# Attention of a gated two-layer block: queries and own keys turned by transposing DMAs, scores for the maximum moved later in the step

## The reference

```python
qkv = (_layernorm(x) @ w_qkv.T)            # 16 heads of 8 columns: q, k, v
k, v = concat([ctx_k, k]), concat([ctx_v, v])   # 64 context rows, then the 64 own rows
attn = softmax((q * 8 ** -0.5) @ k.T)      # for each sequence and head
x = x + tanh(g_xattn[0]) * ((attn @ v) @ w_proj.T + b_proj)
```

## Time and profile before

| | us |
|---|---|
| median of 3 runs | 507.96 (507.57 to 509.46) |
| profiled execution, its own time | 503.36 |
| its span | 501.8 |
| first and last L1525 of the attention | 8.0 and 203.5 |

### The profile page before, as it was taken

How to read it: one execution, slowest core, us unless ns; L and a number is a source line. 1 busy time by engine, 2 the same in 40 slices (tenths; PEclk the granted TensorE clock), 3 DMA queues, 4 the chain that set the end, 5 groups by cost and what they waited for, 6 DMA issues and landing times. The chain is left out here.

```text
span 501.8 us, 21152 instructions
## 1 busy us (share of the span) xinstructions
PE 456.2 (91%) x6983; PEld 359.6 (72%) x6984; DVE 374.9 (75%) x1201; ACT 286.5 (57%) x803; POOL 319.6 (64%) x780
## 2 busy tenths in 40 slices
PE   5799999999999999997987999987998699999998
PEld 3467777766666766764647888874656599998997
DVE  3668989988888989854649766654656688888984
ACT  2378999987888888764324444433333344444431
POOL 3845764576768776756722556667834888988530
PEclk9899999999999999999989999997999699999999
DMA  7930000000000000000144677751000011111001
GB/s 233 413 127 14 27 15 5 5 14 14 12 11 6 11 12 11 14 16 17 58 139 125 189 225 225 224 159 33 22 12 6 22 34 42 37 37 37 22 23 33
DMA packets 22539, 33.62 MB, mean 67 GB/s; under 512 B 5592, under 2 KB 16656, under 8 KB 21968
## 3 DMA queue, kind: packets, MB, share of 16 engines
q0 software_dynamic: 7552, 20.20, 12.6%
q1 hardware_dynamic: 14352, 12.39, 7.6%
q10 hardware_dynamic: 576, 0.26, 0.2%
HBM read 24.82 MB, written 7.86 MB: 65 GB/s over the span
## 5 line engine op out<-in xcount | busy, mean ns | idle before, releaser
L947 DVE TENSOR_REDUCE negm<-PS 128x4 f16<-128x512 f32 x128 | 81.9, 681 | 5.4 <-PE PS L1332 3.0
L689 ACT ACTIVATE pexp<-PS 128x512 f32<-128x512 f32 x128 | 69.6, 595 | 16.1 <-PE PS L1348 12.7
L1684 PE MATMUL PS<-w,vp 128*128 128x128 f32 x512 | 64.0, 279 | 0.0
L1684 PEld LDWEIGHTS PS<-w,vp 128*128 128x128 f32 x512 | 61.2, 196 | 0.0
L1361 PE MATMUL PS<-pexp,vp 128*32 128x64 f32 x2048 | 49.9, 224 | 2.2 <-ACT pexp L689 1.1
L1578 PE MATMUL PS<-xsT,wst 128*128 128x128 f32 x320 | 44.3, 282 | 2.6 <-DVE stack L1185 1.3
L1361 PEld LDWEIGHTS PS<-pexp,vp 128*32 128x32 f32 x2048 | 33.8, 109 | 16.5 <-issue 7.4
L1578 PEld LDWEIGHTS PS<-xsT,wst 128*128 128x128 f32 x320 | 38.8, 191 | 7.0 <-issue 6.0
L584 POOL DMA_DIRECT2D wst<-in_rt_gate_up_dram x40 | 21.6, 540 | 32.6 <-PE PS L1578 22.1
L554 POOL DMA_INDIRECT sorted_x<-VALL,posu x32 | 32.8, 1026 | 13.8 <-issue 8.3
L1278 DVE TENSOR_TENSOR vp<-PS,xnT 128x1024 f32<-128x1024 f32 x32 | 38.7, 1209 | 1.2 <-PE PS L1661 1.2
(11 more groups left out here) (245 smaller groups left out, 1287.8 us busy)
## 6 DMA issues: line engine op xcount, KB each, us to landing
wst<-in_rt_gate_up_dram POOLq DMA_DIRECT2D x40, 256.0 KB, 3.5
xs<-sorted_x SPq DMA_DIRECT2D x40, 64.0 KB, 2.8
sorted_y<-YS POOLq DMA_DIRECT2D x40, 64.0 KB, 3.0
qc<-mT SPq DMA_DIRECT2D x128, 1.0 KB
out_dram<-X SPq DMA_DIRECT2D x32, 64.0 KB
X<-in_x_dram SPq DMA_DIRECT2D x1, 1536.0 KB, 8.8
CK<-in_ctx_k_dram SPq DMA_DIRECT2D x1, 1536.0 KB, 12.0
CV<-in_ctx_v_swapped_dram SPq DMA_DIRECT2D x1, 1536.0 KB, 16.7
```

The costliest lines, as they stand in the source:

```text
L689: nc.scalar.activation(pexp[:, j, :], PS[:, 2 + j % 2, :], ACT.Exp).then_inc(S["exped"], 1)
L947: dve.tensor_reduce(negm[:, a.par, :, j], PS[:, j % 2, :].rearrange("p (g k) -> p g k", g=G), AX.X, ALU.max, negate=True).then_inc(S["maxe ...
L1684: nc.tensor.matmul(PS[:, 6 + y.par, 0:D], z[:, y.par, e, :], w1[:, e * D:e * D + D], start=(e == 0), stop=False)
```

## The change

`turned_on_pe(tile)` is true for the first four tiles. From tile 4 on the queries and the own keys are turned by three transposing DMAs on SP's queue instead of TensorE, and the copies L715 and L986 fall away. The semaphores `stack_turned` take the place of `q_kept`, `k_kept` and `qk_turned`; the next write of the same `stack` buffer (two tiles later) waits for them. The context keys are turned earlier in TensorE's step, into bank 5, and copied between the exponentials. The four small DMAs of the maxima become one. The semaphores of the last three input loads become one.

The order in the step changes too. On TensorE half 0 of the scores for the maximum moves from the step's start to just ahead of the q, k, v matmul; half 1 moves from there to just ahead of the transposes of `oS`; the transpose of the maxima goes behind the first scores by key. On VectorE maxima 0 and 1 go from the start of the step to just ahead of the reciprocal, and maxima 2 and 3 behind the write of the remainder.

```diff
+        def stack_seen(eng, tile):
+            eng.wait_ge(stack_turned[tile.par], 48 * (tile.pair - 1))
+        def stack_freed(eng, tile):
+            if not (tile.turn is None and tile.n < 6):
+                eng.wait_ge(stack_turned[tile.par], 48 * (tile.pair - 2))
...
# SP
+            def turn_stack(s):
+                sp.wait_ge(S["hi_ready"], s.done())
+                sp.wait_ge(S["lo_ready"], s.done())
+                sp.wait_ge(S["scored_t"], s.freed(4, 3, back=16))
+                sp.nop(nofuse=True)
+                sp.dma_start_transpose(qc[:, s.slot], stack[:, s.par, 0, 0:H, :].rearrange("p h c -> p (h c)"))\
+                    .then_inc(stack_turned[s.par], 16)
+                for b in range(2):
+                    own = stack[SEQ * b:SEQ * b + SEQ, s.par, 1, 0:H, :].rearrange("p h c -> p (h c)")
+                    sp.dma_start_transpose(own_half(s.slot)[:, b], own).then_inc(stack_turned[s.par], 16)
             def step(stage):
-                a = stage(3)
+                s, a = stage(1), stage(3)
+                if s and not turned_on_pe(s):
+                    turn_stack(s)
                 if a:
                     sp.wait_ge(S["max_kept"], a.done())
-                    for hg in range(HG):
-                        sp.dma_start(qc[32 * hg + 24:32 * hg + 25, a.slot, :, :],
-                                     mT[HG * hg:HG * hg + G, a.par, :]).then_inc(shift_placed[a.par], 16)
+                    sp.dma_start(qc[24:P:32, a.slot, :, :], mT[:, a.par, :]).then_inc(shift_placed[a.par], 16)
...
# VectorE
-                if a:
-                    max_chunk(a, 0)
-                    max_chunk(a, 1)
                 if l:
...
                 if a:
-                    max_chunk(a, 2)
-                    max_chunk(a, 3)
+                    max_chunk(a, 0)
+                    max_chunk(a, 1)
                 if n:
                     dve.wait_ge(S["o_turned"], n.done())
...
+                if a:
+                    max_chunk(a, 2)
+                    max_chunk(a, 3)
                 if c:
...
# TensorE
-                if a:
-                    scores_for_max(a, 0)
...
                 if a:
-                    scores_for_max(a, 1)
+                    scores_for_max(a, 0)
...
                 if b:
                     average(b, 1)
+                if a:
+                    scores_for_max(a, 1)
                 if n:
```

More of the change, by code:

```diff
@@ L306, in by_seq, with turned_on_pe @@
             return bank.rearrange("p (g b t) -> p b g t", g=G, b=2)
+        def turned_on_pe(tile):
+            return tile.turn is None and tile.n < 4
+        def stack_seen(eng, tile):
[3 more added lines that the diff above has]
+                eng.wait_ge(stack_turned[tile.par], 48 * (tile.pair - 2))
         def bank16(b):
@@ L312, in flamingo_gated_two_layers @@
         TILE_CHUNKS = [(0, 2), (2, 8), (8, NT)]
-        x_in = [sem(f"x_in{c}") for c in range(3)]
-        ck_in = [sem(f"ck_in{c}") for c in range(3)]
-        cv_in = [sem(f"cv_in{c}") for c in range(3)]
+        rest_in = sem("rest_in")
+        x_in = [sem(f"x_in{c}") for c in range(2)] + [rest_in]
+        ck_in = [sem(f"ck_in{c}") for c in range(2)] + [rest_in]
+        cv_in = [sem(f"cv_in{c}") for c in range(2)] + [rest_in]
         consts_in = sem("consts_in")
@@ L331, in flamingo_gated_two_layers @@
         shift_placed = [sem("a_shift_placed0"), sem("a_shift_placed1")]
+        stack_turned = [sem("a_stack_turned0"), sem("a_stack_turned1")]
         for n in "stats moments var_eps copied normed kept xnT_done xnT_kept routed".split():
@@ L383, in arrived @@
                     if tile.n == lo:
-                        eng.wait_ge(sems[c], 16)
+                        eng.wait_ge(sems[c], 16 if c < 2 else 48)
                         eng.nop(nofuse=True)
@@ L700, in step @@
                     if not (w.turn is None and w.n < 2):
-                        act.wait_ge(shift_placed[w.par], 64 * w.pair)
+                        act.wait_ge(shift_placed[w.par], 16 * w.pair)
                     act.wait_ge(S["max_turned"], w.done())
@@ L712, in step @@
                     nc.scalar.copy(xnT[:, f.par, :], PS[:, 4, 0:P]).then_inc(S["xnT_kept"], 1)
-                if s:
+                if s and not turned_on_pe(s):
+                    act.wait_ge(S["ctx_turned"], s.done())
+                    last = nc.scalar.copy(ctx_half(s.slot), by_seq(bank16(5)[:, 0:512]))
+                    last.then_inc(S["ctx_kept"], 1)
+                elif s:
                     act.wait_ge(S["qk_turned"], s.done())
@@ L719, in step @@
                     exp_chunk(b, 3)
-                if s:
+                if s and turned_on_pe(s):
                     act.wait_ge(S["ctx_turned"], s.done())
@@ L724, in step @@
                 if f:
-                    act.wait_ge(S["qk_turned"], f.freed())
+                    if f.turn is None and f.n < 6:
+                        act.wait_ge(S["qk_turned"], f.freed())
+                    stack_freed(act, f)
                     act.wait_ge(S["qkv_done"], f.done())
@@ L782, in gates_in_drain @@
                     shared_gate(3, 1)
-            walk(act, NT, 12, step, lambda: act.wait_ge(ck_in[2], 16), drain=gates_in_drain)
+            walk(act, NT, 12, step, lambda: act.wait_ge(rest_in, 48), drain=gates_in_drain)
             act.wait_ge(S["h_acted"], Tile(EARLY - 1).done(2, 1))
@@ L1052, in products_in_drain @@
                     shared_product(1, 1)
-            walk(dve, NT, 13, step, lambda: dve.wait_ge(x_in[2], 16), drain=products_in_drain)
+            walk(dve, NT, 13, step, lambda: dve.wait_ge(rest_in, 48), drain=products_in_drain)
             chained = [0]
@@ L1323, in scores_for_max @@
                 if half == 0:
-                    pe.wait_ge(S["q_kept"], a.done())
-                    pe.wait_ge(S["k_kept"], a.done())
+                    if turned_on_pe(a):
+                        pe.wait_ge(S["q_kept"], a.done())
+                        pe.wait_ge(S["k_kept"], a.done())
+                    else:
+                        stack_seen(pe, a)
                     pe.wait_ge(S["ctx_kept"], a.done())
@@ L1340, in scores_by_key @@
                 if half == 0:
-                    pe.wait_ge(shift_placed[b.par], 64 * (b.pair + 1))
+                    pe.wait_ge(shift_placed[b.par], 16 * (b.pair + 1))
                 pe.wait_ge(S["exped"], b.freed(4, 2 * half + 1, back=2))
@@ L1440, in step @@
                 past = ro.n + 13 - NT if ro and ro.turn is None else -1
-                if a:
-                    scores_for_max(a, 0)
-                if a:
+                if a and turned_on_pe(a):
                     pe.wait_ge(S["ctx_kept"], a.done())
@@ L1454, in step @@
                     nc.tensor.transpose(PS[:, 6, 0:P], on[:, m.par, :], identf).then_inc(S["on_turned"], 1)
+                if b:
+                    if b.turn is None and b.n == 0:
+                        keep_busy(14, 7)
+                    scores_by_key(b, 0)
                 if c:
@@ L1458, in step @@
                                         ident16[:]).then_inc(S["max_turned"], 1)
[L1459 to L1463, removed]
+                if s and not turned_on_pe(s):
+                    pe.wait_ge(S["ctx_stacked"], s.done())
+                    turn_stack(s, 2, 5, 0, "ctx_turned")
+                elif s:
                     if s.turn is None and s.n == 0:
@@ L1537, in step @@
                     average(b, 1)
+                if a:
+                    scores_for_max(a, 1)
                 if n:
                     pe.wait_ge(S["o_kept"], n.done())
-                    if s:
+                    if s and not turned_on_pe(s):
+                        pe.wait_ge(S["ctx_kept"], s.done())
+                    elif s:
                         pe.wait_ge(S["k_kept"], s.done())
@@ L1544, in step @@
                     last.then_inc(S["o_turned"], 1)
-                if s:
-                    if s.turn is None and s.n < 3:
+                if s and turned_on_pe(s):
+                    if s.n < 3:
                         keep_busy(5, 7)
```

## The result

The changed kernel takes 584.38 us (median of 4 runs, 577.0 to 592.35) against 508.71 us for the kernel before beside it. Forecast were 542 us. The time lies just inside the range of 525 to 585 us, but the loss is 76 us where 34 were forecast.

What follows compares the result with a forecast made beforehand. The attention was taken as bound by TensorE before and by a 7.33 us chain of waits after; 13.5, 17.8 and 2.4 us added 34 to 503.4, giving 537 us profiled and 542 us median, range 525 to 585.

Steps and rivals of the forecast that it cites:

- The ring: Attention steps: one chain of waits through TensorE, VectorE and ScalarE sets the pace, 7.33 us a step; chance 0.76.
- The waits: Per attention step: VectorE about 1 us ahead of the reciprocal; TensorE 0.4 ahead of half 1, about 1.3 later.
- The sum at full clock: Steps 6 to 34: 13.5 us lost in ten written-out steps, 17.8 in sixteen loop steps, 2.4 at the end; 33.7 together.
- the drain: The two steps after the loop: 1.2 us lost in each, 2.4 us together.
- the last rival, the clock: TensorE in the attention: pauses halve its clock in stretches, 29 steps growing by up to 100 us; chance 0.02.
- The sign for it: TensorE's busy share from 48 to 96 us would fall from 99% to under 85%.
- a kernel bound by its DMAs: Rival on SP's queue: issue of the three transposes over 5.8 us decides, 572 to 640 us; chance 0.12.
- The DMAs: SP's three transposing DMAs a tile: about 3 us of issue, hidden, with no wait for them.
- The limit behind it: SP's queue: the maxima's small DMA follows the transposes, whose issue may take up to 5.8 us a tile.
- No gain from TensorE's saved work: TensorE in the attention: the 0.45 us a step saved on transposes of q and k buys nothing.

Runs made afterwards that it cites:

- The order alone: Kernel before with only the changed order of scores and maxima, q and k still turned on TensorE: 557.29 us against 492.86, 1.128.
- the order back: Changed kernel with scores for the maximum, their maxima and the maxima's transpose in the old order, transposing DMAs kept: 506.8 us, 1.023 of the kernel before.
- the output first: Changed kernel with only the transposes of the output moved ahead of half 1 of the scores: median 551.72 us.
- With fillers: Changed kernel plus 12 idle matmuls ahead of the transpose of the maxima and 4 ahead of half 1: 535.28 us, 1.087 of the kernel before.
- half 0 in between: Changed kernel, DMAs kept, half 0 behind the first scores by key, the rest ordered as before: 504.16 us, 1.017 of the kernel before.

## Why the prediction was wrong

- **The ring: right.** Summed from the trace of before it was 7.33 us a step; the changed kernel took 7.12 us at full clock. This isn't errors that cancel: the links measure 0.46 us (0.53 in the sum), 1.34 (1.34), 1.04 (1.04), 0.84 (0.83), 1.33 (1.34) and, from the turned maxima to the next half 0, 2.11 (0.85 + 1.40). The order alone took 7.25 us, and 7.33 once the router's matmul is in the step as it is in the rows summed. The waits came where they were named: 1.09 us ahead of the reciprocal (about 1 forecast), 0.19 us ahead of half 1 (0.4), 0.86 + 0.23 us ahead of the turned maxima and the context transposes (1.3). One reading was wrong without consequence: in the step of the earlier trace rows ScalarE waited twice and not once, 0.18 us and 0.25 us for the context keys (L722). That the order and not the DMAs makes the ring is shown by the order alone (7.25 us), the order back, and the output first (0.60 us less).
- **The sum at full clock: nearly right.** 33.7 us were forecast. With fillers, the loss was 42.4 us by the medians and 38.7 us by the spans of the two traces (532.4 and 493.7 us), which can be divided. The q, k, v matmuls of tiles 5, 15 and 31, with fillers (L1565) and in before (L1525):

```profile
38.19 0.91 PE L1565 MATMUL PS<-wqkv,xnT 128*128 128x384 f32 x2
...
111.96 0.91 PE L1565 MATMUL PS<-wqkv,xnT 128*128 128x384 f32 x2
...
233.62 0.91 PE L1565 MATMUL PS<-wqkv,xnT 128*128 128x384 f32 x2
```

```profile
39.06 0.91 PE L1525 MATMUL PS<-wqkv,xnT 128*128 128x384 f32 x2
...
99.06 0.91 PE L1525 MATMUL PS<-wqkv,xnT 128*128 128x384 f32 x2
...
201.09 0.91 PE L1525 MATMUL PS<-wqkv,xnT 128*128 128x384 f32 x2
```

  For tiles 5 to 15 the loss was 10 x (7.38 - 6.00) = 13.8 us (13.5 forecast), for 15 to 31 16 x (7.60 - 6.38) = 19.5 us (17.8). 6.2 us lie behind tile 31's matmul (from there to the end of the span 298.8 us against 292.6), where 2.4 had been summed for the drain, and 0.9 us were gained ahead of tile 5. The terms of the sum were sound, then, the drain's apart.
- **What failed is the last rival, the clock, with its chance of 0.02.** It was dismissed because "the gaps here are under 1.1 us and repeat; the loop of before has gaps too and the full clock". That compared the length of single gaps. What before and after differ in is the sum of gaps a step: TensorE was busy 97.77 of 104 us in before, and 4.62 of 6 us here ahead of the fall. The forecast itself said under 85% busy, and didn't ask what that does to the clock. It costs some 44 us here, about as much as the ring. The price was of the right order: at half the clock a loop step is 9.99 us, 2.4 us more than the 7.60 us of the loop with fillers; up to 3.4 us were worked out. The sign for it was of no use in the form given: from 48 to 96 us TensorE was busy 87% (41.76 of 48 us) and not under 85%, since the halved clock fills the time; only the 77% at full clock shows the gaps.
- **That the time lies within the range is luck.** Its upper end of 585 us had been set for a kernel bound by its DMAs, which this one isn't.
- **The DMAs: hidden, as forecast.** 3.7 us of issue where 3 were taken, no wait for them. The limit behind it is real, but past it a step costs far more than the sum gives (9 to 12 us each between 40 and 140 us, where 7.5 were worked out), and the clock falls too.
- **No gain from TensorE's saved work: right,** and worse than that: in the order back and with half 0 in between TensorE has less work and also waits for DMAs, the clock falls after such gaps, and both are slower than before. How much of that is the waits and how much the clock wasn't separated.

On the clock, the Trainium skill ("TensorE: Matmul & The Clock Gate", What's actually happening) says that throttled is the default state and activity releases it. The fillers agree: the same program with 16 idle matmuls more a step, and the granted clock goes from 0.63 to 1.00 between 96 and 200 us.

## What to carry to other kernels

When an order is changed, write down the ring of waits through all engines and add it up from start-to-start times of the old trace; here it gave 7.33 us for a step that took 7.12. Then take the busy share of TensorE that follows from it, and price the case that the clock halves before giving it a small chance: an engine that is no longer the bound can become it again at half speed. Idle matmuls in a real wait cost 0.07 us a step here and gave back 44 us; on the engine's own path they gained nothing that could be measured.

## What was not expected of the hardware

- The transposing DMA of 64 partitions by 512 takes as long to issue on SP (1.25 us) as the one of 128 by 512 (1.19 us), with half the data; the longest took 2.1 us. The plain issue of the earlier trace rows took 0.57 us.
- One lands 2.4 to 2.5 us after its issue. The figure of 1309 ns for a 128x128 block in the Trainium skill ("VectorE: DVE Perf Modes", The three transpose paths) gives an estimated 5.2 us for the four blocks of the queries if they are taken one after the other. The trace has them landed in half of that, so the figure doesn't add up block by block, and the measurement decides. Whether the blocks overlap or the figure holds a fixed part, no run here shows.
- The same kernel of before took 508.7 us on one chip and 493 to 496 us on three others. In the traces of two of them part of it is in the loop, 6.69 us a step against 6.38.
